# Expert products in token-major form, their sum on GpSimd, and four PSUM banks for the first distances

## The reference

```python
# 1: attention by squared distance, over one batch of 512 tokens
dist_sq = maximum(sq[:, :, None] + sq[:, None, :] - 2 * einsum('bie,bje->bij', x, x), 0)
x1 = x + softmax(-gamma * dist_sq) @ norm(x)
# 2: cross attention, 16 heads of 8, onto 154 context rows, with ALiBi slopes
x2 = x1 + (softmax(q @ k.T / sqrt(8) + slope * (i - j)) @ v) @ Wo.T + bo
# 3: eight experts, each token through the two with the highest logits, unweighted
mask = one_hot(top_k(softmax(h @ router_w.T + router_b), 2)).sum(-2)      # h = norm(x2), mask (b, s, 8)
out = einsum('bse,ehd,bsd->bsh', mask, expert_w, h) + einsum('bse,eh->bsh', mask, expert_b)
x3 = x2 + out
```

## Time and profile before

| | |
|---|---|
| median of 3 runs | 230.81 us (228.4 to 230.9) |
| profiled execution | 232.36 us, span 230.6 us from first to last instruction |
| busy | PE 197.7 us (86%), DVE 156.1 (68%), ACT 108.8 (47%), POOL 34.8 (15%) |
| chain that ended last | PE 53%, DVE 21%, ACT 9%, DMA 6%, issue 6%, POOL 3% |
| granted TensorE clock | mean 0.985 of full speed |
| instructions | 3497 |

### The profile page before, as it was taken

The page is one execution under the profiler, slowest core; times in us unless marked ns, Lnnn a source line. Parts: engine busy times, 40 slices in busy tenths (PEclk is TensorE's granted clock), DMA queues, the critical chain, the costliest instruction groups (busy, mean ns, idle before and its releaser), DMA issues.

```text
span 230.6 us, 3497 instructions
## 1 busy us (share of the span) xinstructions
PE 197.7 (86%) x1178; PEld 101.4 (44%) x1194; DVE 156.1 (68%) x433; ACT 108.8 (47%) x206; POOL 34.8 (15%) x98
## 2 busy tenths in 40 slices
PE   7659969887676899979999999899898668999894
PEld 2226924563221343835434459433243232345572
DVE  3472494569996288687788787767689424578872
ACT  2257625802057977338673545593132267721210
POOL 4612045510400022040100002200000003003000
PEclk9997997999999999999999999999999999999999
DMA  5999230590024501020631000203601110000011
GB/s 156 321 192 354 61 88 0 189 209 7 0 51 157 127 1 43 7 55 0 190 86 25 19 0 11 53 35 110 178 0 43 35 30 0 0 4 1 0 45 45
DMA packets 23158, 16.89 MB, mean 73 GB/s; under 512 B 10676, under 2 KB 21772, under 8 KB 23052
## 3 DMA queue, kind: packets, MB, share of 16 engines
q1 hardware_dynamic: 23140, 16.67, 26.8%
HBM read 11.29 MB, written 5.37 MB: 72 GB/s over the span
## 4 chain that ended last, share of the span: by engine, by line
PE 53%; DVE 21%; ACT 9%; DMA 6%; issue 6%; POOL 3%; SPq 0%; DVEq 0%; ACTq 0%; POOLq 0%
PE bank L1135 11%; DVE nm L803 11%; PE bank L910 7%; PE bank L1062 6%; PE bank L1011 4%; PE bank L966 4%; PE bank L950 4%; PE bank L1041 4%; PE bank L1122 2%; ACT w L592 2%; PE bank L1056 2%; PE bank L1089 2%; ACT ptail L644 2%; DMA q_scratch<-qpart 2%; DVE rm L720 2%
## 5 line engine op out<-in xcount | busy, mean ns | idle before, releaser
L803 DVE TENSOR_REDUCE nm<-bank 128x3 f32<-128x462 f32 x88 | 50.0, 620 | 14.1 <-PE bank L1011 13.8
L644 ACT ACTIVATE pt<-bank 128x512 f32<-128x512 f32 x64 | 35.8, 598 | 20.3 <-PE bank L1041 15.5
L1011 PE MATMUL bank<-kA,qs 128*128 128x308 bf16 (+1 forms) x172 | 29.5, 263 | 7.0 <-DVE nm L803 5.5
L1135 PE MATMUL bank<-ym,ewT 128*128 128x512 f32 (+1 forms) x80 | 32.8, 512 | 0.0
L883 DVE TENSOR_TENSOR ym<-bank,y3T 128x512 f32<-128x512 f32 (+1 forms) x40 | 21.9, 580 | 7.7 <-PE bank L1122 5.3
L1011 PEld LDWEIGHTS bank<-kA,qs 128*128 128x128 bf16 x172 | 12.8, 97 | 31.9 <-DVE nm L803 22.2
L950 PE MATMUL bank<-y1Tg,y1T 128*128 128x512 f32 x32 | 18.5, 663 | 6.6 <-ACT w L584 5.8
L485 POOL TENSOR_SCALAR ve<-mv 128x4 f32<-128x4 f32 (+1 forms) x13 | 2.5, 196 | 128.1 <-DVE mv L696 127.9
L1041 PE MATMUL bank<-qs,kB 128*128 128x512 bf16 x59 | 20.2, 382 | 1.8 <-ACT pt L644 1.0
L584 ACT ACTIVATE w<-bank,snsq,sgn 128x512 f32<-128x512 f32 x16 | 12.2, 774 | 14.8 <-DVE rm L720 14.8
L905 PE MATMUL bank<-idle 128*128 128x512 bf16 x54 | 15.9, 437 | 1.9 <-DVE idle L688 1.5
(11 more groups left out here) (130 smaller groups left out, 267.5 us busy)
## 6 DMA issues: line engine op xcount, KB each, us to landing
qs<-q_scratch SPq DMA_DIRECT2D x16, 192.0 KB, 3.6
q_scratch<-qpart SPq DMA_DIRECT2D x4, 384.0 KB, 2.4
xs<-in_x_dram SPq DMA_DIRECT2D x4, 256.0 KB, 8.0
vm<-in_vm_ones_dram SPq DMA_DIRECT2D x1, 1024.0 KB, 12.7
q_scratch<-qpart SPq DMA_DIRECT2D x4, 256.0 KB, 2.1
kA<-k_scratch SPq DMA_DIRECT2D x8, 120.0 KB, 2.8
kB<-k_scratch SPq DMA_DIRECT2D x8, 120.0 KB, 2.5
out_dram<-ob SPq DMA_DIRECT2D x3, 256.0 KB, 2.6
```

What stands on the lines that cost most here:

```text
L644: nc.scalar.activation(dst, ST[n % 2][:, :], ACT.Exp).then_inc(exps, 1)
L803: v.tensor_reduce(negated[:, GROUP * g:GROUP * g + heads], MX[n % 2][:, 0:heads * J].rearrange("p (s j) -> p s j", s=heads), AX.X, ALU.max ...
L1011: last = mm(MX[n % 2][:, at * J:(at + heads) * J], qs[:, b % 2, a, tile(t)], kA[:, s:s + heads, a, 0:J], start=True, stop=True)
L1135: last = mm(YMS[b][p][:, at], ewT[:, e, :], ym[:, e, at], start=False, stop=(e == E - 1))
```

## The change

Two parts of the program are written anew, and the order tables with them.

**The expert layer becomes token-major.** The stationary operand is now a tile of 128 turned tokens (`y3T`), the moving one the weights of four experts side by side (512 columns); one float32 matmul gives the products of 128 tokens with four experts. There are two halves of experts for each of four tiles, so eight such matmuls a batch. `spread` goes, and with it its matrix and the load of it. `select` now multiplies the product, read from PSUM, by a mask column per expert (`maskf`, float32, one new DVE instruction per `route`). In the last batch DVE does so for experts 0 to 3, and ACT for experts 4 to 7 (`weigh`, four copies of 128 columns with a scale). `bias` is the experts' bias matmul, whose result DVE adds to x2. `total`, on POOL, sums the nine slabs of `prod` for each tile by four additions of 512, 256, 128 and 128 columns, which write the output tile. The last two tiles are summed by two DVE reductions of 9 x 128 elements instead (`store:3.1`). `fT` and its transposes go.

**The first batch's distances** use four banks (`DB`: A0, A1, MX[1], ST[0]) instead of two, and for batches 0 and 1 the copy scaled by 2*gamma is made on DVE from the first copy instead of on ACT from PSUM.

```diff
-        y1T:0 sqT:0 dist:0.0 dist:0.1 dist:0.2 dist:0.3 keys:0 probs:0.0 probs:0.1 y1T:1 probs:0.2 sqT:1
...
+        y1T:0 sqT:0 dist:0.0 dist:0.1 dist:0.2 dist:0.3 probs:0.0 keys:0 probs:0.1 probs:0.2 probs:0.3 self:0.0
...
-    "y1T:0": 16, "probs:0": 1, "probs:1": 16, "maxima:0": 2, "y2T:1": 4, "scores:1": 8, "y3T:1.0": 4, "y2T:3": 3,
-    "divide:2.1": 2, "scores:3": 3, "mask:3": 2,
+    "y1T:0": 16, "y2T:0": 7, "query:0": 5, "probs:1": 6, "maxima:0": 12, "y2T:1": 4, "query:1": 1, "scores:0": 10,
+    "divide:0.1": 1, "wo:0.0": 1, "experts:1": 5, "divide:2.1": 8, "scores:3": 1, "y3T:2.0": 1, "wo:3.1": 3,
+    "y3T:3.1": 1,
 }
 
...
+        DB = [(A0, A1, MX[1], ST[0])] + [(A0S[b], A1S[b]) * 2 for b in range(1, B)]
...
+            def total(b, t):
+                n = T * b + t + 1
+                if b < B - 1:
+                    pool.wait_ge(mx_free, expert_fill(b, 2 * t + 2))
+                else:
+                    pool.wait_ge(mx_free, expert_fill(b, 0) + t + 1)
+                    pool.wait_ge(weighed, t + 1)
+                g.tensor_tensor(prod[:, t, 0:4, :], prod[:, t, 0:4, :], prod[:, t, 4:8, :], ALU.add).then_inc(halved, 1)
+                pool.wait_ge(halved, n)
+                g.tensor_tensor(prod[:, t, 0:2, :], prod[:, t, 0:2, :], prod[:, t, 2:4, :], ALU.add).then_inc(quartered, 1)
+                pool.wait_ge(quartered, n)
+                g.tensor_tensor(prod[:, t, 0, :], prod[:, t, 0, :], prod[:, t, 1, :], ALU.add).then_inc(summed, 1)
+                pool.wait_ge(summed, n)
+                pool.wait_ge(x2b_ready, b + 1)
+                if b >= 2:
+                    pool.wait_ge(stored[b % 2], ONE * (b // 2))
+                g.tensor_tensor(ob[:, b % 2, t], prod[:, t, 0, :], prod[:, t, E, :], ALU.add).then_inc(out_ready, 1)
+
...
                     act.wait_ge(gamma_ready, 2)
                 act.wait_ge(y1T_ps, b + 1)
                 copy(y1T[:, :], A0S[b][:, :]).then_inc(y1T_sb, 1)
-                nc.scalar.activation(y1Tg[:, :], A0S[b][:, :], ACT.Copy, scale=gam2[:, :]).then_inc(y1T_sb, 1)
+                if b >= 2:
+                    nc.scalar.activation(y1Tg[:, :], A0S[b][:, :], ACT.Copy, scale=gam2[:, :]).then_inc(y1T_sb, 1)
 
             def sqT_(b, _):
                 act.wait_ge(sqT_ps, b + 1)
...
                     if b >= 2:
                         act.wait_ge(pT_ps, T * (b - 2) + t + 1)
-                    nc.scalar.activation(w[:, b % 2, t, :], (A0S, A1S)[t % 2][b][:, :], ACT.Relu, bias=snsq[:, t:t + 1],
+                    nc.scalar.activation(w[:, b % 2, t, :], DB[b][t][:, :], ACT.Relu, bias=snsq[:, t:t + 1],
                                          scale=sgn[:, :]).then_inc(w_relu, 1)
...
+            def weigh(b, t):
+
+                n = expert_fill(b, 2 * t + 1)
+                act.wait_ge(out_ready, T * (b - 1) + t + 1)
+                act.wait_ge(mask_ready, b + t // 2 + 1)
+                act.wait_ge(mx_full, n + 1)
+                for e in range(EH):
+                    last = nc.scalar.activation(prod[:, t, EH + e, :], MX[n % 2][:, e * D:(e + 1) * D], ACT.Copy,
+                                                scale=maskf[:, t, EH + e:EH + e + 1])
+                last.then_inc(weighed, 1)
 
             walk("scalar", {"y1T": y1T_, "sqT": sqT_, "dist": dist, "soft": soft, "probs": probs, "keys": keys,
...
+            def y1T_(b, _):
+                if b == 0:
+                    dve.wait_ge(gamma_ready, 2)
+                dve.wait_ge(y1T_sb, 2 * b + 1)
+                v.tensor_scalar(y1Tg[:, :], y1T[:, :], gam2[:, :], None, ALU.mult).then_inc(y1g_sb, 1)
...
+                done(v.tensor_scalar(maskf[:, at, :], rank[:, at, :], 1.5, None, ALU.is_lt))
...
             def select(b, q):
-                p, e = q // E, q % E
-                at = span(b, p)
-                if e == 0:
-                    dve.wait_ge(y3T_sb, b + p + 1)
+
+                t, h = (q // 2, q % 2) if b < B - 1 else (q, 0)
+                n = expert_fill(b, 2 * t + h)
+                if h == 0:
+                    settle()
                     if b >= 1:
-                        dve.wait_ge(f_ps, b)
-                n = spread_fill(b, q)
+                        dve.wait_ge(out_ready, T * (b - 1) + t + 1)
                 dve.wait_ge(mx_full, n + 1)
-                v.tensor_tensor(ym[:, e, at], MX[n % 2][:, at], y3T[:, at], ALU.mult).then_inc(mx_free, 1)
+                v.tensor_tensor(prod[:, t, EH * h:EH * (h + 1), :], MX[n % 2][:, :].rearrange("p (e d) -> p e d", d=D),
+                                maskf[:, t, EH * h:EH * (h + 1)].unsqueeze(2).broadcast_to([P, EH, D]),
+                                ALU.mult).then_inc(mx_free, 1)
+
+            def bias(b, p):
+                at = tiles(b, p)
+                dve.wait_ge(bias_ps, b + p + 1)
+                if b >= 1:
+                    dve.wait_ge(out_ready, T * b)
+                v.tensor_tensor(prod[:, at, E, :], YMS[b][p][:, span(b, p)].rearrange("p (t d) -> p t d", d=D),
+                                x2[:, b % 2, at], ALU.add).then_inc(x2b_ready, 1)
 
             def store(b, p):
-                at = tiles(b, p)
-                dve.wait_ge(fT_ps, b + p + 1)
-                if b >= 2:
-                    dve.wait_ge(stored[b % 2], ONE * (b // 2))
-                v.tensor_tensor(ob[:, b % 2, at], YMS[b][p][:, span(b, p)].rearrange("p (t d) -> p t d", d=D),
-                                x2[:, b % 2, at], ALU.add).then_inc(out_ready, 1)
-
-            walk("vector", {"stats1": stats1, "y1": y1_, "dist": dist, "rowmax": rowmax_,
+
+                dve.wait_ge(x2b_ready, B + 1)
+                dve.wait_ge(mx_free, expert_fill(b, 0) + T)
+                dve.wait_ge(weighed, T)
+                dve.wait_ge(stored[b % 2], ONE * (b // 2))
+                for t in rows_of(b, p):
+                    last = v.tensor_reduce(ob[:, b % 2, t, :], prod[:, t, :, :].rearrange("p e d -> p d e"), AX.X, ALU.add)
+                last.then_inc(last_ready, 1)
+
+            walk("vector", {"y1T": y1T_, "stats1": stats1, "y1": y1_, "dist": dist, "rowmax": rowmax_,
                   "invert": invert, "gather": gather, "y2": y2_, "weights": weights, "keys": keys, "query": query, "maxima": maxima,
...
 
 
-                pe.wait_ge(y1T_sb, 3 * (b + 1))
+                pe.wait_ge(y1T_sb, y1T_count(b + 1) - 1)
+                pe.wait_ge(y1g_sb, min(b + 1, 2))
                 for t in range(k, k + 1):
-                    if t >= 2:
+                    if t >= 2 and b >= 1:
                         pe.wait_ge(w_relu, T * b + t - 1)
-                    mm((A0S, A1S)[t % 2][b][:, :], y1T[:, tile(t)], y1Tg[:, :], start=True, stop=False)
-                    mm((A0S, A1S)[t % 2][b][:, :], ones16[:, :], sqT[:, :], start=False, stop=True).then_inc(dist_ps, 1)
+                    if t == 1:
+                        pe.wait_ge(y1T_sb, y1T_count(b + 1))
+                    mm(DB[b][t][:, :], y1T[:, tile(t)], y1Tg[:, :], start=True, stop=False)
+                    pe.wait_ge(y1T_sb, y1T_count(b + 1))
+                    mm(DB[b][t][:, :], ones16[:, :], sqT[:, :], start=False, stop=True).then_inc(dist_ps, 1)
 
...
-            def spread_(b, q):
-                p, e = q // E, q % E
-                n = spread_fill(b, q)
-                if e == 0:
+            def experts(b, q):
+
+                t, h = q // 2, q % 2
+                n = expert_fill(b, q)
+                if q == 0:
                     pe.wait_ge(mT_sb, min(b + 2, B))
                     pe.wait_ge(mx_free, n)
-                    warm(MX[n % 2], f"spread:{b}.{q}")
-                    pe.wait_ge(mask_sb, b + p + 1)
+                    warm(MX[n % 2], f"experts:{b}")
                     if b == 0:
-                        pe.wait_ge(expert_in, 3 * ONE)
-                pe.wait_ge(mx_free, n - 1)
-                mm(MX[n % 2][:, span(b, p)], spread[:, e, :], maskT16[:, span(b, p)], start=True,
-                   stop=True).then_inc(mx_full, 1)
-
-            def experts(b, q):
-                p, e = q // E, q % E
-                at = span(b, p)
-                if e == 0:
-                    pe.wait_ge(mask_sb, b + p + 1)
-                    if b == 0:
-                        pe.wait_ge(bias_ready, 1)
-                        pe.wait_ge(expert_in, 3 * ONE)
-                    mm(YMS[b][p][:, at], ebias[:, :], maskT16[:, at], start=True, stop=False)
-                pe.wait_ge(mx_free, spread_fill(b, q) + 1)
-                last = mm(YMS[b][p][:, at], ewT[:, e, :], ym[:, e, at], start=False, stop=(e == E - 1))
-                if e == E - 1:
-                    last.then_inc(f_ps, 1)
...
+            def bias(b, p):
+                pe.wait_ge(mask_sb, b + p + 1)
+                if b == 0:
+                    pe.wait_ge(bias_ready, 1)
+                for t in rows_of(b, p):
+                    last = mm(YMS[b][p][:, tile(t)], maskT16[:, tile(t)], ebias[:, :], start=True, stop=True)
+                last.then_inc(bias_ps, 1)
```

225 lines of the change are left out of this document (112 added, 113 removed).

## The result

The changed kernel takes 233.23 us (median of 4 runs, 232.84 to 236.12), the kernel before 230.75: ratio 1.0161, 95% interval 1.0096 to 1.0225 (the two medians alone give 1.011). So it is slower; whether by the two per cent that the prediction set as its limit stays unclear, since the interval lies on both sides of 1.02. The prediction said 223.5, range 219.5 to 229.5. The profiled execution took 232.84 us (span 230.8, clock 0.986).

What follows compares the result with a forecast made beforehand. Each stage was taken to have its own bound: PE, DVE, or latency in batch 3's query and the end. Gains 4.3 + 2.2 + 1.6 + 0.5 + 1.7 minus 3.0 made 7.3 us: 223.5 us, range 219.5 to 229.5.

Steps and rivals of the forecast that it cites:

- Term 5: POOL's sums: 2.9 us a tile, and contention with DVE costing 3.0 us (0 to 8.8).
- Lock: Rival: every two-input DVE instruction waits for the running POOL instruction; 8.8 us lost, 229.3 us in all; chance 0.21.
- Term 1: The start: four banks and a new order bring batch 0's gather and scores 4.3 us sooner.
- Term 2: PE work of the expert layer: broadcasts and four turnings per batch go; 2.2 us gained.
- Term 3: Batch 3's query: shorter latency from self:3 to the maxima; 1.6 us gained before contention.
- Over 20 is lock: Sign: self:3 to batch 3's maxima takes 17 to 19 us; over 20 means two-input DVE instructions wait for POOL.
- Term 4: The end, last values to store: 3.0 us gained, minus 1.3 for experts ahead of the values; 1.7 net.
- POOL did not end last: Rival judged: POOL ends last at the end, with sums of 5.5 us instead of 2.9; 235 us; chance 0.04.
- Does not do what it says: Rival: PE's freed time turns into other waits everywhere, no gain; 231 us; chance 0.04.
- Clock: Rival: batch 0's self runs at half clock and eats most of the start's gain; 227.5 us; chance 0.06.

Runs made afterwards that it cites:

- the second trace: The kernel before, unchanged, profiled once more: that execution took 229.02 us at clock 1.000; ratio 1.0066 against itself.
- e6: The changed kernel with the first batch's distances back in two banks instead of four: 234.69 us, ratio 1.0183 to the kernel before.
- e1: The changed kernel with POOL's additions cut to 4 of 128 columns, the sums left out of the output: 224.41 us, ratio 0.9705 to the kernel before.
- e8: The changed kernel with its two closing reductions over nine neighbouring numbers instead of numbers 128 apart (output not right): 234.2 us in one execution.
- e3: The changed kernel with POOL's sums of batches 0 and 1, and the bias sums they need, moved to other places: 230.75 us, ratio 1.0002 to the kernel before.
- e7: The changed kernel with each POOL sum made by eight additions of 128 numbers instead of four larger ones: 232.05 us, ratio 1.0045 to the kernel before.
- e2: The changed kernel with POOL's additions replaced by one-input copies of as many elements, sums left out: 226.43 us, ratio 0.9792 to the kernel before.
- e5: The changed kernel with POOL's additions replaced by one-input copies of about the additions' length, sums left out: 230.47 us, ratio 0.9992 to the kernel before.
- b1: The changed kernel with POOL's early batches' sums moved, bias order edited, and closing additions instead of reductions: 228.76 us, ratio 0.9900 to the kernel before.
- e4: The changed kernel with DVE's two closing reductions replaced by four additions over both tiles: 234.11 us, ratio 1.0137 to the kernel before.
- b2: As b1, with one POOL sum of batch 2 also waiting for the first ranking of batch 3: 228.37 us, ratio 0.9901 to the kernel before.

## Why the prediction was wrong, point by point

**What bounds the kernel.** Right in the main: the latency from y2 to the maxima of batch 3 and the tail decide, and there the change lost 4.9 and 2.6 us. A third place was not reckoned with, y3 of batch 2 (below).

**Term 5, the sums, is the step that failed.** "Contention: 3.0 us lost (0 to 8.8)". Removing the sums gives 8.7 us of span. These 5.7 us too many are the largest part of the miss of 9.7. The rival "Lock" (8.8) comes out almost to the tenth, but that is luck in its parts. In batch 3's stretch it had 4.5 us (y2 1.0, ranking 1.6, query parts 1.9) and found are 4.9 (2.0, 1.8, 1.1). At the end it had 4.3 and found are 2.6: y3:3.1 1.0, the rankings 1.4 and 0.6 instead of 1.9 each, less 0.4 that a wait for PE covers. Between the scores of batch 3 and the last values it had nothing and found are 1.6, since y3 of batch 2 takes 3.10 us instead of 1.12. The rest is 0.15 lost between the maxima and the scores of batch 3 and 0.5 gained ahead of the end of `self:3`. I had seen one y3 instruction of four at 1032 ns and taken one wait per place. The other three kept 334 ns, and the trace has no second POOL instruction behind the one of 1.09 us; beside a queue of sums each DVE instruction waits for one POOL instruction. It was followed by something that I did not reckon with: PE's idle 2.65 us and the lower clock behind it, about 1 us on the projection. That this 1 us cost time is not shown: ACT had its query part done at 150.08 us, and DVE, held up by its own turns, took the next one only at 150.95. POOL's duration was well put, 2.9 to 3.1 us a tile against 2.9, though its 512 columns took 1.26, not 1.09.

The Trainium skill (SBUF — State Buffer, section Who interferes with whom) states that a DVE instruction with two SBUF inputs contends with a GpSimd instruction that reads SBUF, that one in a 2-port mode does too, for the whole instruction, and that one with at most one SBUF input outside these modes does not. These traces agree: comparisons, query parts and y2 wait, also beside copies that read one input; maxima, and products out of PSUM (0.69 us in all kernels), don't. In which mode y2 ran no row shows. I gave that rule a chance of 0.21, against a row that was no evidence against it.

**Term 1, the start: 4.3 us forecast.** The event times were right (gather 24.74 for 24.6, first maxima 46.02 for 45.5, scores 66.51 for 67). The base was not: the earlier trace rows showed the dips, and I took them as a risk for the changed kernel instead of as a cost inside the trace that I measured against. Against the second trace the start is worth 2.2 us at the first scores and 1.0 at the scores of batch 1. Of the total, 1 us is the banks' (e6).

**Term 2, PE's work: 2.2 us forecast**, 3.0 found (lead 1.0 at the scores of batch 1, 4.0 at the end of `self:3`, against the second trace). The new orders lie in these 3.0 too, and no run parts them from the lighter experts. In the forecast the four turnings are 0.7 us by the earlier trace rows (2.7 us for 16), not 0.5.

**Term 3, batch 3's query: 1.6 before contention.** Without sums 18.2 us from `self:3` to the maxima (17.8 forecast), 19.3 in the second trace: 1.1 gained. The sum was right by luck, its parts were not: up to the last query part it took 11.5 us (10.0 forecast, 11.4 in the second trace), from there to the maxima 6.8 (7.8 forecast, 8.0 by the earlier trace rows, 7.9 in the second trace). So the new order of y2 and query gained nothing up to there. What was gained lies behind it, where the write of the last part took 2.4 us in e1 and 3.7 in the second trace; why is open. "Over 20 is lock": it was 23.1.

**Term 4, the end: 1.7 gained.** Wrong for two reasons beside contention. The reductions take 2.04 us each where I had 1.3 from a maximum over 512 numbers in a row; e8 shows 1.3 for a row and 0.74 more for the stride: 1.5 us for both. And without sums the tail is 27.9 us, not 25.3: 2.6 more, of which the reductions are 1.5 and 1.1 have no place in one row. With sums it is 30.5, against 28.2 before. The forecast of 1.3 us for the experts ahead of the values holds within a few tenths (17.8 us from the scores of batch 3 to the last values in e1, 16.7 before).

**The sum again.** Between the second trace and e1, the kernel without sums, the lead at the end of `self:3` is 3.5 us where Terms 1 and 2 had 6.5 (3.0 short). From there to the scores of batch 3, 2.4 are gained where Term 3 had 2.1; then 1.1 lost for 1.3, and 0.3 gained in the tail for 3.0 (2.7 short). So 223.5 + 5.7 (contention) + 3.0 - 0.3 - 0.2 + 2.7 = 234.4 us; measured 233.23. The rest is the base: the second trace's execution took 229.02 us, 1.7 under the median before, the changed kernel's 232.84, 0.4 under its own, so the comparison of traces holds 1.3 us that the medians do not. The rival "Lock" at 229.3 had the mechanism and failed by Terms 1, 2 and 4. POOL did not end last (its last sum ends at 224.85, 24.5 us behind the last values where 20.8 were forecast; DVE ends at 228.48). "Does not do what it says" fell by the lead of 4 us. "Clock" named the wrong place: the clock held in the start and fell in batch 3's query.

## What to carry to other kernels

Before work goes to an idle GpSimd, look at what VectorE does at that time: beside SBUF-to-SBUF instructions each of them pays one GpSimd instruction, beside reductions and products out of PSUM it paid nothing here (0.53 us a maximum, 0.69 a product, with and without sums). Put it where VectorE reads PSUM (e3: y2 back at 1.11 us), and look at what it then falls on, as `mcat` there. Keep the instructions short as long as GpSimd has slack (e7). Before a trace is made the base of a sum, read its clock row: a dip in a stage is a cost of that execution, and the change does not give it back.

## What the runs showed of the hardware that was not expected

- DVE and POOL take turns on SBUF, one instruction for one, also when POOL copies with a single input (e2, e5). That a row of DVE instructions lasts as long as as many POOL instructions, counted from start to start (1.72 us for 1.74, 2.57 for 2.59, 3.07 for 3.08), is from these runs.
- The delay goes both ways: POOL's 512-column addition took 1.71 us in b1 beside DVE additions, 1.26 otherwise.
- A DVE reduction of 9 x 128 float32 numbers took 2.04 us with a stride of 128 and 1.3 in a row.
- A POOL addition of 512 columns took 1.26 us where inputs and output lie in `prod`, and 1.09 for `x1b`.
- PE idled 2.65 to 2.67 us for y2 of batch 3 in the changed kernel, e4, e8 and e6, and the granted clock of the 5 us from 147 on was 0.77, 0.53, 0.66 and 0.72 (1.00 would be 2.4 GHz throughout, 0.50 would be 1.2). In e5 it idled 2.16 us and in e1, e2, e3, e7, b1 and b2 less, and the clock stayed at 1.00 there.
- The unchanged kernel, timed against itself, gave a ratio of 1.0066 (1.0004 to 1.0129): the clock's dips, which the first trace of the kernel before has and the second has not, go with 3.3 us of span, as much as the differences between some of these kernels.
